# First attention's opening in a one-core decoder kernel: the order of stacks, scalings and maxima

## The reference

```python
def _L0_xattn_ref(x, y, Wq, bq, Wkv, bkv, q_gamma, q_beta, k_gamma, k_beta, Wproj, bproj):
    q = (x @ Wq.T + bq).reshape(B, N, H, D).transpose(0, 2, 1, 3)
    kv = (y @ Wkv.T + bkv).reshape(B, M, 2, H, D).transpose(2, 0, 3, 1, 4)
    k, v = (kv[0], kv[1])
    q = _layernorm(q, q_gamma, q_beta) * SCALE
    k = _layernorm(k, k_gamma, k_beta)
    attn = jax.nn.softmax(jnp.einsum('bhnd,bhmd->bhnm', q, k), axis=-1)
    out = jnp.einsum('bhnm,bhmd->bhnd', attn, v)
...
x = x + jnp.tanh(g_xattn[0]) * _L0_xattn_ref(_layernorm(x, axis=-1), ctx_1024, ...)
```

## Time and profile before

| what | value |
|---|---|
| median of 3 runs | 777.44 us (772.36 to 777.78) |
| time of the profiled execution | 777.46 us |
| its span in the trace | 775.7 us |
| PE busy | 720.0 us, 93% of the span |
| DVE, ACT, POOL busy | 556.0, 358.5, 334.4 us |
| PE in 40 slices of 19.4 us | 5 7 7 9 9 9 and so on |
| TensorE clock granted, same slices | 9 7 7 9 9 9 and so on |

### The profile page before, as it was taken

One profiled execution on the slowest core, in us unless ns is written; L12 is line 12 of the kernel. 1 busy time (PEld: TensorE's weight loads), 2 busy tenths in 40 slices (PEclk: granted clock), 3 DMA queues, 4 the chain that ended last, 5 costly groups with the idle time before them and its releaser, 6 DMA issues.

```text
span 775.7 us, 14479 instructions
## 1 busy us (share of the span) xinstructions
PE 720.0 (93%) x5654; PEld 537.4 (69%) x5654; DVE 556.0 (72%) x1086; ACT 358.5 (46%) x530; POOL 334.4 (43%) x411
## 2 busy tenths in 40 slices
PE   5779999999999998999999999999999989999996
PEld 4656666666877776666776666766767656887794
DVE  4767887774887777886668767587966787677444
ACT  2657767665434335545544555345454545120300
POOL 3283534410333114666556566566665674100000
PEclk9779999999999999999999999999999999999999
DMA  8100000000500040000000000000000000000000
GB/s 178 17 1 2 3 1 2 2 2 9 210 1 0 1 106 4 2 2 1 2 1 1 2 2 2 1 2 1 1 2 1 2 1 1 1 8 1 8 8 7
DMA packets 25554, 11.57 MB, mean 15 GB/s; under 512 B 11832, under 2 KB 24200, under 8 KB 25360
## 3 DMA queue, kind: packets, MB, share of 16 engines
q1 hardware_dynamic: 24480, 10.59, 5.3%
q10 hardware_dynamic: 1008, 0.07, 0.1%
HBM read 10.06 MB, written 0.52 MB: 14 GB/s over the span
## 4 chain that ended last, share of the span: by engine, by line
PE 74%; DVE 18%; issue 4%; ACT 3%; DMA 1%; SPq 0%; DVEq 0%; ACTq 0%
PE ps L1689 71%; DVE o L1416 2%; PE ps L1700 2%; ACT v L598 1%; DVE mx L1092 1%; DVE pmax L1400 1%; DVE ysum L1548 1%; DVE pmax L1403 1%; DVE kql L1391 1%; DMA raw<-in_L_xattn_Wproj_dram 1%; DVE rs_t L962 1%; PE ps L1793 1%; DVE rs_t L969 1%; DVE cn L1353 1%; DVE xnC L1203 1%
## 5 line engine op out<-in xcount | busy, mean ns | idle before, releaser
L837 ACT ACTIVATE p<-ps 128x1024 f32<-128x1024 f32 x96 | 96.3, 1025 | 129.8 <-PE ps L1689 129.8
L573 POOL TENSOR_TENSOR acc<-p 128x256 f32<-128x256 f32 x128 | 92.7, 755 | 97.7 <-ACT p L837 97.7
L1689 PE MATMUL ps<-p,v 128*64 128x256 f32 (+1 forms) x1280 | 130.2, 386 | 1.8 <-DVE o L1417 1.3
L1689 PE MATMUL ps<-kqh 64*128 64x256 f32 (+1 forms) x640 | 105.1, 363 | 10.8 <-ACT v L598 4.6
L579 POOL TENSOR_TENSOR acc<-acc,p 128x256 f32<-128x256 f32 x128 | 89.8, 733 | 49.7 <-ACT p L837 49.7
L1400 DVE TENSOR_REDUCE pmax<-ps 128x2 f32<-128x1024 f32 x64 | 78.2, 1222 | 34.4 <-PE ps L1689 33.4
L1092 DVE TENSOR_REDUCE mx<-ps 128x1 bf16<-128x512 f32 x128 | 82.5, 687 | 26.5 <-PE ps L1689 25.9
L1689 PEld LDWEIGHTS ps<-p,v 128*64 128x64 f32 (+1 forms) x1280 | 63.3, 125 | 50.8 <-issue 18.8
L534 POOL TENSOR_SCALAR q<-qst,rmask 128x256 fp32r<-128x256 f32 x64 | 58.7, 936 | 59.3 <-ACT qst L598 59.3
L1689 PEld LDWEIGHTS ps<-kqh 64*128 64x128 f32 x640 | 58.9, 190 | 35.7 <-issue 29.1
L702 ACT ACTIVATE p<-ps 128x1024 f32<-128x1024 f32 x64 | 65.5, 1025 | 23.1 <-PE ps L1689 21.4
(11 more groups left out here) (285 smaller groups left out, 1593.4 us busy)
## 6 DMA issues: line engine op xcount, KB each, us to landing
w<-in_L_ffn_W_dram SPq DMA_DIRECT2D x1, 2048.0 KB, 12.1
wt<-in_L_ffn_W_dram SPq DMA_DIRECT2D x4, 512.0 KB, 6.2
ctx_all<-in_ctx_dram SPq DMA_DIRECT2D x4, 256.0 KB, 5.7
raw_kv<-in_L_xattn_Wkv_dram SPq DMA_DIRECT2D x1, 1024.0 KB, 4.9
raw<-in_L_ffn_B_dram SPq DMA_DIRECT2D x9, 64.0 KB
xr<-in_x_dram SPq DMA_DIRECT2D x4, 128.0 KB, 4.0
raw_q<-in_L_xattn_Wq_dram SPq DMA_DIRECT2D x1, 512.0 KB, 5.9
wout<-in_L_xattn_Wout_dram SPq DMA_DIRECT2D x1, 512.0 KB, 7.2
```

Of the source, the lines that this page charges most:

```text
L573: ins = pool.tensor_tensor(acc1[:, at], p1[:, s, 0, at], p1[:, s, 1, at], ALU.add)
L837: act.activation(p1[:, g % 2, u, :], bank(2 * (n % 2), 2), ACT.Exp, scale=SCALE1).then_inc(a_exp1.sem, 1)
L1689: return pe.matmul(o, lhsT, rhs, start=start, stop=stop)
```

## The change

It reorders the opening and changes no number that is computed.

- PE: `prep_spread(0)` goes ahead of `context_values0(0)` and `prep_var(1)`. All stacks of quads 0 to 2 follow in one piece. `prep_spread(1)` goes behind `rows0(0)` and `weights_turn(3)`; `context_values0(2)` and `context_values0(3)` go behind the last maxima of quad 1, just ahead of the loop. The wait for all values (`d_v0` 4) moves from `stack_q(2)` to `stack_q(3)`, since these values now use bank 6 just before.
- DVE: `scale0` is split into the scaling, the root (`root0`) and the widening (`spread0`). The root of batches 2 and 3 goes in three pieces among the maxima of quad 0, its widening behind them, `scaled0(1)` behind the second maximum of quad 1, `values0_in(2)` and `values0_in(3)` behind the last.
- ACT: `prep_final(1)` goes behind the stacks of quads 0 to 2; `prep_final(2)` and `prep_final(3)` go into the loop, behind the last `exp0` of turns 1 and 3.
- POOL: `masked0(1)` goes ahead of `rest(1)`; `rest(2)` goes behind `masked0(5)`, `rest(3)` behind `masked0(7)`.

```diff
@@ POOL
             rest(0)
-            masked0(0)
-            rest(1)
-            rest(2)
-            rest(3)
-            for q in range(1, AQ):
+            for q in range(AQ):
                 masked0(q)
+                if q == 1:
+                    rest(1)
+                if q in (5, 7):
+                    rest((q - 1) // 2)
@@ ACT
             prep_final(0)
-            prep_final(1)
...
             stack_k(0)
-            prep_final(2)
-            prep_final(3)
             stack_q(1)
             stack_k(1)
             stack_k(2)
+            prep_final(1)
...
                     exp0(4 * q + 3)
+                    if q == 1:
+                        prep_final(2)
+                    if q == 3:
+                        prep_final(3)
@@ DVE
             scale0(0)
+            root0(3, True)
+            spread0(0)
+            scaled0(0)
             values0_in(0)
-            scaled0(0)
             scale0(1)
             values0_in(1)
-            scaled0(1)
-            values0_in(2)
-            values0_in(3)
...
+            for n in range(8):
+                row_max0(0, n)
+                if n == 1:
+                    root0(1, True)
+                if n in (3, 5):
+                    root0(1, False)
+            spread0(1)
+            for n in range(8):
+                row_max0(1, n)
+                if n == 1:
+                    scaled0(1)
+            values0_in(2)
+            values0_in(3)
@@ PE
-            context_values0(0)
             tokens_turn0(1)
             keys0(2)
             keys0(3)
             queries0(1)
+            prep_spread(0)
+            context_values0(0)
             prep_var(1)
-            prep_spread(0)
             context_values0(1)
...
             stack_k(0)
-            prep_spread(1)
-            context_values0(2)
-            pe.wait_ge(d_knq.sem, B)
+            pe.wait_ge(a_kqc.sem, 2)
             stack_q(1)
             stack_k(1)
             stack_k(2)
-            context_values0(3)
-            pe.wait_ge(d_v0.sem, B)
+            pe.wait_ge(d_v0.sem, 2)
             stack_q(2)
...
             weights_turn(3)
+            pe.wait_ge(a_kst.sem, 3)
+            prep_spread(1)
             for n in (4, 5):
                 first_maxima(n)
                 weights_turn(n)
-            pe.wait_ge(a_kst.sem, 3)
+            pe.wait_ge(d_knq.sem, B)
             scores0(0)
             first_maxima(6)
             weights_turn(6)
             scores0(1)
             first_maxima(7)
+            pe.wait_ge(a_wT.sem, WT_GROUPS)
+            context_values0(2)
+            context_values0(3)
```

More of the change, by code:

```diff
@@ L1048, in scale0, with root0, spread0 @@
                 dve.wait_ge(d_vh.sem, n + 1)
-                rsqrt(vh, y, tmp, columns=False)
+            def root0(steps, guess):
+                vh, y, t = (a[:, :] for a in rs_wide)
+                if guess:
+                    then(dve.tensor_scalar(t.bitcast(I32), vh.bitcast(I32), 1, None, ALU.arith_shift_right))
+                    then(dve.tensor_scalar(y.bitcast(I32), t.bitcast(I32), -1.0,
+                                           float(RSQRT_MAGIC - (1 << 22) - (1 << 30)), ALU.mult, ALU.add))
+                for n in range(steps):
+                    then(dve.tensor_tensor(t, y, y, ALU.mult))
+                    then(dve.tensor_tensor(t, t, vh, ALU.mult))
+                    then(dve.scalar_tensor_tensor(out=y, in0=t, scalar=1.5, in1=y, op0=ALU.add, op1=ALU.mult))
+            def spread0(n):
+                y = rs_wide[1]
                 if n == 1:
@@ L1119, in residual0 @@
                                          op1=ALU.add).then_inc(d_xA.sem, 1)
-            for q in range(2):
-                for n in range(8):
-                    row_max0(q, n)
+            for n in range(8):
[11 more added lines that the diff above has]
+            values0_in(3)
             def half_rsqrt(vh, y, t, half):
@@ L1806, in stack_q @@
                 if q == SLOTS - 1:
-                    pe.wait_ge(a_wT.sem, WT_GROUPS)
+                    pe.wait_ge(d_v0.sem, B)
                 if q >= SLOTS - 1:
```

## The result

| what | before | after |
|---|---|---|
| median of 20 runs each | 775.28 us (772.16 to 780.04) | 779.60 us (777.58 to 781.65) |
| ratio after to before | | 1.0051, 95% interval 1.0035 to 1.0066 |
| span of the profiled execution | 775.7 us | 778.3 us |
| PE busy | 720.0 us | 719.6 us |

The change makes the kernel 0.5% slower, and the interval is clear of 1, so the loss is real though small. The forecast was 781.5 from 777.46, which is a ratio of 1.0052. It also took differences under 1% for unmeasurable; with 20 runs each the interval is narrower than 0.2% to either side.

The account below looks back on a forecast made before the run. PE was taken to bound the kernel, busy 93% of the span and 74% of the last chain. From 777.46, -0.2 for the opening and +4.2 for two loop waits gave 781.5 us, 0.5% slower; own range 779 to 784.

Parts of the forecast that it names:

- The loop pieces: Turns 2 and 4: `prep_final(2)` and `(3)` delay ACT's copies, so PE waits at `stack_k(5)` and `stack_k(7)`; two times 2.1, +4.2 us.
- 2.5 us between the two exponentials less 0.37 of slack: End of turn 1: `prep_final(2)` delays the copy of `stack_q(5)` by 2.5 us; PE's slack is 0.37, leaving a 2.1 us wait.
- PE's idle time in turns 2 and 4 could be followed by half clock: Loop: PE's clock may fall to half behind the waits, as in the opening, and those turns grow by more; no size given.
- The opening as a sum: Ahead of the loop: the 9.5 us lead at the first weights is eaten by DVE and PE waits; worth -0.2 us.
- The road to the first weights: Opening: an earlier `prep_spread(0)` brings the first stack to 33.4 and the first turned weights to 40.4, a 9.5 us lead.
- The blocked operation: Opening, DVE: `rest(1)` on POOL at 42.2 to 44.0 holds up the root's second Newton step, 1.4 us.
- PE has nothing else in its list, DVE nothing either: Second `prep_spread`: twelve transposes follow the first widening copy at once, 2.0 us counted; DVE idle about 2 us.
- 1.5 us at the upper end of its range: Opening: transposes and `context_values0(3)` at half clock would cost 0.6 + 0.9 us more; only in the range.
- Hidden pieces: Rival, 18%: ACT is 2.1 us ahead at the end of turns 1 and 3, so the waits vanish; 777.3 us.
- The lead lives: Rival, 7%: DVE's stretch between first weights and loop packs tighter, 5.5 to 9.5 us of lead stay; 772 to 776.
- Masks block the root: Rival, 17%: in the opening each POOL mask holds up a DVE root operation for its whole 0.90; +4.4, 785.9 us.

Follow-up runs that it names:

- first: The changed kernel with `prep_final(2)` and `prep_final(3)` out of the loop, directly behind `exp0(1)`: 776.55 against 774.59 us for the kernel before, ratio 1.0017.
- fourth experiment: The changed kernel with the eight activations of `prep_final(2)` and `(3)` one per turn, `rest(2)` and `rest(3)` later: 773.67 against 774.59 us before, ratio 0.9988.
- second: The kernel before with only `prep_final(2)` and `(3)` moved into the loop, with `rest(2)` and `rest(3)`: 775.91 against 774.59 us before, ratio 1.0033.
- doubled piece: The changed kernel with four more activations in `prep_final(2)`, 5.0 instead of 2.5 us of ACT expected: 781.42 us against 778.78 before, one run each.
- second trace: The changed kernel run again without edits for one more trace: 783.13 us, with the kernel before at 778.78, one run each.
- `rest(1)` first: The changed kernel with `rest(1)` directly behind `masked0(0)` on POOL instead of behind `masked0(1)`: 779.14 against 775.11 us for the kernel before, ratio 1.0043.
- order on PE: The changed kernel with quad 1's first two maxima ahead of `prep_spread(1)` and `weights_turn(3)` ahead of `rows0(0)`: 779.52 against 775.11 us before, ratio 1.0055.
- `rest(1)` later: The changed kernel with `rest(1)` behind `masked0(2)` on POOL instead of behind `masked0(1)`: 778.66 against 774.59 us for the kernel before, ratio 1.0059.

## Why the prediction was right

**The loop pieces.** The step that carried the forecast, two waits at `stack_k(5)` and `stack_k(7)`, came as written: place, releaser and count. Its size was 2.1 each; the turns grew by 1.80 and 1.76 (9.55 less 7.75, 9.55 less 7.79), so 3.6 instead of 4.2. The term that was too large is "2.5 us between the two exponentials less 0.37 of slack". The four activations take 2.40 (75.88 to 78.28), and before the second exponential had itself waited some 0.25 for its scores; now they are long there. So the copy came 2.13 later against `exp0(7)`, not 2.5. The slack that remained is the 0.06 between the end of the copy (79.54) and the start of the matmul (79.60), so 0.31 of the 0.37 were usable, and 2.13 less 0.31 is 1.82. The opposite edits agree: without the pieces the growth is gone (first and fourth experiment), in the old opening it is there (second), and with more work in the piece it grows one for one (turn 2 of the doubled piece, 11.94 against 9.55).

**What the prediction named and did not price.** It said that PE's idle time in turns 2 and 4 could be followed by half clock. This happened behind five of sixteen such waits in eight traces of kernels with the pieces in the loop: behind four of fifteen of 1.6 us each, turn 3 or 5 took 9.43 to 9.47 instead of 7.9, and behind the one of 4.04 10.57. On average that is some 0.8 us for two waits, which belongs to the 4.0 of the ratio. So the forecast's total of +4.0 met the measured +4.0 (+2.7 to +5.1 by the interval) partly by luck: the waits were 0.6 too large in the sum, and the clock's 0.8 was not in it. The 3.6 from the waits, the 0.8 from the clock and what the next paragraph finds for the opening make some 4.6. These shares come from few executions and hold no better than a microsecond.

**The opening as a sum.** -0.2 was forecast. By d at `stack_k(4)`, which excludes both waits, the three traces of the changed kernel have 45.23, 45.07 and 44.33 against 44.90: +0.3, +0.2 and -0.6. Two experiments with the same opening, single activations and doubled piece, have 45.46 and 45.63: +0.6 and +0.7. The mean of the five is +0.2. The sum is right within what executions differ by; the sign stays open.

**The opening step by step.** Here errors cancelled:

| point | forecast | measured |
|---|---|---|
| first stack | 33.4 | 32.62 |
| first turned weights | 40.4 | 39.06 |
| first of the remaining maxima | 41.3 | 40.03 |
| maxima of quad 0 done | 49.55 | 47.90 |
| next maximum | 52.3 | 52.49 |
| four products done | 55.85 | 55.55 |
| stack of quad 3 | 62.85 | 62.69 |
| `scores0(4)` | 67.75 | 67.84 |

- The forecast counts from the trace before, whose first copy to `rexp` began at 25.22; here it began at 24.82. So 0.4 us of each difference in the table is the start of the execution: by d the maxima of quad 0 are 1.25 early, the next maximum is 0.6 late, and the stack of quad 3 is 0.2 late.
- The road to the first weights came out 1.3 us shorter, 0.9 by d (14.24 against 15.2). In ten more traces with this piece of code the first weights stand at d 13.7 to 15.4, so the forecast is within what executions differ by. ACT began `prep_final(0)` at 27.98 instead of 28.5, POOL's subtraction ended at 32.48 instead of 33.0, and PE was then free within 0.17 us.
- The blocked operation is as forecast in this trace: 1.96 us beside `rest(1)`, 1.6 above its own 0.36. In the second trace it was 0.45. Putting the subtraction first took 1.5 us out on DVE (`rest(1)` first). That the forecast counted the collision as certain was lucky for the first trace, and harmless in the second, where the later start cost as much.
- The step that failed is "PE has nothing else in its list, DVE nothing either" at the second `prep_spread`. PE has `rows0(0)` and `weights_turn(3)` in front of it, both behind the last maximum of quad 0. They ran at half clock, 48.04 to 49.26, and the twelve transposes took 2.77 instead of the 2.0 that was counted. DVE stood still for 3.57 us instead of about 2. That ate the 1.65 us by which the maxima were early. Placing maxima under the transposes took the wait away and gave about 1.2 of it back (order on PE).
- The half clock was longer than the two stretches before: from 40.7 to 54.3 us the windows view gives 0.50. The prediction had it only as 1.5 us at the upper end of its range.

**The rivals.** *Hidden pieces*: out, by the changed kernel and the four experiments on these pieces. *The lead lives*: out for this change, but as a possibility right. The lead at the first weights was 10.9. Three places that ate it could be mended: 2.2 at the subtraction (1.5 of it the collision), some 1.2 at PE's order, and 3.1 at the values, in single traces. With all three mended the loop starts 5.6 us earlier than before (d 31.09 against 36.73), and with the `prep_final` pieces split too the kernel is 0.6% faster. *Masks block the root*: out. Beside masks a root operation took 0.51 to 0.57 instead of 0.36, and not every one; that is 0.15 to 0.2 more, never the 0.90 of a mask. The two widening copies took 1.43 beside masks (`rest(1)` first) instead of 1.02, but 1.08 beside masks in the trace before.

The Trainium skill, "SBUF — State Buffer", section "Who interferes with whom", has a DVE instruction with two SBUF inputs and a GpSimd instruction that reads SBUF contend, the loser blocked in full. Beside the subtraction, which has two SBUF inputs itself, seven traces agree (1.83 to 1.91 us of POOL, 1.88 to 2.03 us of DVE). In four more the operation began later within the subtraction and took 0.45 to 0.86. In all eleven it ended 0.21 to 0.23 us after the subtraction. Beside the masks, whose tensor input is one, the measurement differs and decides: part of a mask's time, not all.

## What to carry to other kernels

- When the engine at its limit shares a buffer with another engine's copy, ask how long the list of that other engine in front of the copy may get. Here the margin was 0.3 us, a piece of 2.4 us cost 1.8 twice, and the same work in eight single pieces cost nothing.
- A lead in the opening is worth what arrives at the first full loop turn. Follow it over each hand-over on the way; each of three places took 1 to 3 us. With two of them mended and the loop pieces split the kernel was 0.25% faster than before, with the third 0.6%.
- Work with a hand-over in it (the values through one bank) is cheaper inside a full loop turn than in front of it, if its result is needed only later: there only the bound engine's own part remains.

## What the runs showed of the hardware

- TensorE's clock can fall to its half level behind a single wait of 1.6 us in an otherwise full loop: in the four cases seen it fell 0 to 1.4 us after the end of the wait, was half for 3.4 us, and the turn grew by 1.5 to 1.6 us, about the price of the wait itself. In eleven like cases, in the same kernel too, it stayed full. In the same stretch of five traces without such waits it never fell. I had not put this into the sum.
- The root operation on DVE that began while POOL's subtraction ran (two SBUF inputs, 0.36 us alone) ended 0.21 to 0.23 us after the subtraction in eleven traces, however much of it was left, and took 0.45 to 2.03 us. Beside POOL's masks, which read one tensor of SBUF, it took 0.57 at most.
- Executions differ by 2 to 3 us in stretches whose code the change doesn't touch. Ahead of the opening the first copy to `rexp` began at 21.95 to 25.22. The four matmuls `ctxT,wt` there took 3.75 us in the kernel before (from 12.80 on) and 1.95 in the trace with `rest(1)` later. That looks like half clock, but the windows view has the granted clock at 1.00 over both, so the cause is not shown. Beyond 200 us the granted clock over 100 us was 0.97 in one execution and 1.00 in another. A difference of the size tested here has to be read from the place of the change, or timed in many runs.
